# Full attention: PSUM banks and distances of the two matmul streams that run ahead

## The reference, cut to what matters

```
x = x + attn(_layernorm(x), Wq, bq, Wk, bk, Wv, bv, Wo, bo)      # _L1_attn_b_ref
def proj(W, b):
    return (jnp.einsum('btc,oc->bto', x, W) + b).reshape(Bb, Tt, H, D).transpose(0, 2, 1, 3)
q = _rope(proj(Wq, bq)); k = _rope(proj(Wk, bk)); v = proj(Wv, bv)
scores = jnp.einsum('bhtd,bhsd->bhts', q, k) / jnp.sqrt(D)
attn = jax.nn.softmax(scores, axis=-1)
out = jnp.einsum('bhts,bhsd->bhtd', attn, v)
out = out.transpose(0, 2, 1, 3).reshape(Bb, Tt, C)
return jnp.einsum('btc,oc->bto', out, Wo) + bo
```

## Time and profile before

| | us |
|---|---|
| median of 3 runs | 4485.8 |
| lowest, highest | 4483.82, 4503.86 |
| profiled execution, its own time | 4470.18 |
| span of its trace | 4468.4 |
| full attention in it, first maxima matmul to last values (3464 to 4118) | 654 |
| part with scores (3500.3 to 4118) | 617.7 |
| one frame of 64 slots, full clock | 78.8 |

### The profile page before, as it was taken

One profiled execution on the slowest core, in us unless ns is written; L12 is line 12 of the kernel. 1 busy time (PEld: TensorE's weight loads), 2 busy tenths in 40 slices (PEclk: granted clock), 3 DMA queues, 4 the chain that ended last, 5 costly groups with the idle time before them and its releaser, 6 DMA issues. The chain is left out here.

```text
span 4468.4 us, 60003 instructions
## 1 busy us (share of the span) xinstructions
PE 3753.4 (84%) x19225; PEld 2607.0 (58%) x19288; DVE 2864.8 (64%) x5347; ACT 1912.2 (43%) x3864; POOL 1567.3 (35%) x1463
## 2 busy tenths in 40 slices
PE   5888878799499999988898588885886888888898
PEld 3555557688488888877787244443663333333566
DVE  6676557565555555547565478777885566664898
ACT  3454543343355555453343344532221355555232
POOL 4565526444566655436443111100001443330000
PEclk8898989899799999989899688997998799998999
DMA  6987912454100000002454200000001544450000
GB/s 171 270 240 229 271 40 71 145 163 150 43 11 12 17 13 11 1 17 73 152 168 142 65 19 19 19 1 15 0 0 36 102 98 84 96 102 16 9 10 19
DMA packets 221651, 348.37 MB, mean 78 GB/s; under 512 B 34632, under 2 KB 126266, under 8 KB 215226
## 3 DMA queue, kind: packets, MB, share of 16 engines
q1 hardware_dynamic: 198714, 260.66, 19.8%
q0 software_dynamic: 22656, 84.24, 8.3%
HBM read 166.29 MB, written 169.87 MB: 75 GB/s over the span
## 5 line engine op out<-in xcount | busy, mean ns | idle before, releaser
L2771 DVE TENSOR_REDUCE ab_nmx<-banks 128x1 f32<-128x512 f32 x512 | 334.7, 686 | 208.1 <-PE banks L2587 207.3
L2713 ACT ACTIVATE ab_pt<-banks 128x512 f32<-128x512 f32 x512 | 273.7, 600 | 90.2 <-PE banks L2597 77.4
L1664 POOL TENSOR_TENSOR lb_pq<-lb_pq,lb_rr 128x512 f32<-128x512 f32 x192 | 203.9, 1065 | 307.1 <-DVE lb_rr L1543 304.1
L2597 PE MATMUL banks<-ab_qT,ab_kT 49*128 49x512 f32 x512 | 227.5, 491 | 54.9 <-ACT ab_pt L2713 52.9
L1418 ACT ACTIVATE lb_pq<-banks,lb_nmx 128x256 f32<-128x256 f32 x384 | 178.9, 471 | 220.5 <-DVE lb_nmx L1538 217.6
L2587 PE MATMUL banks<-ab_kT,ab_qT 48*128 48x512 f32 x512 | 235.4, 508 | 30.7 <-DMA ab_kT<-ab_spill 19.1
L1538 DVE TENSOR_REDUCE lb_nmx<-banks 128x2 f32<-128x512 f32 x192 | 131.5, 685 | 185.2 <-PE banks L1270 184.2
L2597 PEld LDWEIGHTS banks<-ab_qT,ab_kT 49*128 49x128 f32 x512 | 92.2, 194 | 261.6 <-ACT ab_pt L2713 158.5
L634 POOL DMA_INDIRECT mb_xi<-moe_ys,moe_b_place x64 | 63.6, 995 | 390.3 <-DVE mb_uT L2045 342.7
L2825 POOL DMA_DIRECT2D ab_kT<-in_ab_ones x4 | 2.1, 548 | 525.0 <-POOLq L2978 525.0
L566 POOL TENSOR_TENSOR da_pt<-da_pt,w_da_tri 128x384 f32<-128x384 f32 x128 | 144.8, 1131 | 111.0 <-ACT da_pt L350 110.8
(11 more groups left out here) (561 smaller groups left out, 11480.3 us busy)
## 6 DMA issues: line engine op xcount, KB each, us to landing
moe_xs<-zero SPq DMA_DIRECT2D x71, 512.0 KB, 11.1
moe_ys<-zero SPq DMA_DIRECT2D x71, 512.0 KB, 10.9
moe_a_w_raw<-in_moe_w SPq DMA_DIRECT2D x48, 512.0 KB, 3.9
moe_b_w_raw<-in_moe_w SPq DMA_DIRECT2D x48, 512.0 KB, 3.8
da_spill<-da_hi SPq DMA_DIRECT2D x128, 128.0 KB, 2.4
ab_spill<-ab_hi SPq DMA_DIRECT2D x128, 128.0 KB, 2.4
da_qT<-da_spill POOLq DMA_DIRECT2D x32, 384.0 KB, 7.3
da_kT<-da_spill POOLq DMA_DIRECT2D x32, 384.0 KB, 10.3
```

The lines of the kernel that those rows point to most:

```text
L1664: nc.gpsimd.tensor_tensor(pq[:, n % RING, :, :], pq[:, n % RING, :, :], bcast(rr[:, n % RING, :], 2, 2 * P), ALU.mult).then_inc(s_p, 1)
L2597: nc.tensor.matmul(ps[:, EXP_BANK + n % 3, :], kT[b % 2][r:r + AB_ROWS + 1, p, j * P:(j + 1) * P], qT[b % 2][r:r + AB_ROWS + 1, p, :], sta ...
L2713: nc.scalar.activation(pt[:, s % RING, :], ps[:, EXP_BANK + s % 3, :], ACT.Exp, scale=AB_D ** -0.5).then_inc(s_e, 1)
L2771: nc.vector.tensor_reduce(nmx[:, g % 2, col:col + 1], ps[:, MAX_BANK + n % 3, :], op=ALU.max, axis=AX.X, negate=True).then_inc(s_mx, 1)
```

## The change

Two banks for maxima and four for scores instead of three and three. The waits follow the number of banks, TensorE issues scores one slot further ahead (s+3), and LEAD goes from 37 to 38. Nothing else is different.

```diff
-    LEAD = 37
+    LEAD = 38
     RING = 8
     NV = NS // 4
-    MAX_BANK, EXP_BANK, SUM_BANK, ODD_BANK = 0, 3, 6, 7
+    MAX_BANK, EXP_BANK, SUM_BANK, ODD_BANK = 0, 2, 6, 7
+    NMAX, NEXP = 2, 4
...
-                    if n >= 3:
-                        pe.wait_ge(s_mx, n - 2)
-                    nc.tensor.matmul(ps[:, MAX_BANK + n % 3, :], ...
+                    if n >= NMAX:
+                        pe.wait_ge(s_mx, n - NMAX + 1)
+                    nc.tensor.matmul(ps[:, MAX_BANK + n % NMAX, :], ...
...
-                    if n >= 3:
-                        pe.wait_ge(s_e, n - 2)
-                    nc.tensor.matmul(ps[:, EXP_BANK + n % 3, :], ...
+                    if n >= NEXP:
+                        pe.wait_ge(s_e, n - NEXP + 1)
+                    nc.tensor.matmul(ps[:, EXP_BANK + n % NEXP, :], ...
...
-                    if 0 <= s + 2 < NS:
-                        scores(s + 2)
+                    if 0 <= s + NEXP - 1 < NS:
+                        scores(s + NEXP - 1)
...
-                        nc.scalar.activation(pt[:, s % RING, :], ps[:, EXP_BANK + s % 3, :], ACT.Exp,
+                        nc.scalar.activation(pt[:, s % RING, :], ps[:, EXP_BANK + s % NEXP, :], ACT.Exp,
...
-                        nc.vector.tensor_reduce(nmx[:, g % 2, col:col + 1], ps[:, MAX_BANK + n % 3, :], op=ALU.max,
+                        nc.vector.tensor_reduce(nmx[:, g % 2, col:col + 1], ps[:, MAX_BANK + n % NMAX, :], op=ALU.max,
```

More of the change, by code:

```diff
@@ L2584, in maxima @@
                             pe.wait_ge(s_stack[i], stack_all * (2 * b + g // 2 + 1))
-                    if n >= 3:
-                        pe.wait_ge(s_mx, n - 2)
-                    nc.tensor.matmul(ps[:, MAX_BANK + n % 3, :], qT[b % 2][r:r + AB_ROWS, p, qt * P:(qt + 1) * P],
+                    if n >= NMAX:
+                        pe.wait_ge(s_mx, n - NMAX + 1)
+                    nc.tensor.matmul(ps[:, MAX_BANK + n % NMAX, :], qT[b % 2][r:r + AB_ROWS, p, qt * P:(qt + 1) * P],
                                      kT[b % 2][r:r + AB_ROWS, p, :], start=True, stop=True).then_inc(s_m, 1)
@@ L2594, in scores @@
                         pe.wait_ge(s_shift[n // 16 % 2], shift_all * (n // 32 + 1))
-                    if n >= 3:
-                        pe.wait_ge(s_e, n - 2)
-                    nc.tensor.matmul(ps[:, EXP_BANK + n % 3, :], kT[b % 2][r:r + AB_ROWS + 1, p, j * P:(j + 1) * P],
+                    if n >= NEXP:
+                        pe.wait_ge(s_e, n - NEXP + 1)
+                    nc.tensor.matmul(ps[:, EXP_BANK + n % NEXP, :], kT[b % 2][r:r + AB_ROWS + 1, p, j * P:(j + 1) * P],
                                      qT[b % 2][r:r + AB_ROWS + 1, p, :], start=True, stop=True).then_inc(s_s, 1)
```

## The result

The changed kernel takes 4548.99 us in the median of 4 runs, against 4494.83 us in the median of 4 of the kernel before: ratio 1.0123, 95% interval 1.0099 to 1.0147, about 54 us slower. The direction was forecast, at half the size: 28 us and 4514 were predicted, and the range ended at 4536.

A forecast was written before the change was run, and what follows sets the result against it. TensorE's strict order, with each stop of its queue, was taken as the bound. Terms 20 + 5.4 + 1.5 + 3 - 2.7 = +27, with small waits +28, on the median 4485.8 gave 4514 us; 8-in-10 range 4497 to 4536.

The forecast's parts named there:

- plain groups: Four slots without odd jobs: third maxima wait for the first reduction, 2.74 us becomes 3.34, +0.60 each.
- v job: Slots 26 to 29: the job's first load follows the later third maxima, +0.85 us, nothing behind recovers it.
- end of the frame: Slots 62 to 65: the turn beside GpSimd's operation ends earlier, maxima of slot 65 go sooner, -0.3 us.
- tail: The 38 slots without maxima: values to values 2.22 us instead of 2.60, -2.7 us in all, from 0 to -8.
- heads, out and qk groups: Groups with these jobs: a job or ScalarE's emptying separates the pairs long enough, so the change costs 0.
- Before the first scores: Maxima ahead of any scores go 0.79 us apart instead of 0.60: +3 us, from 0 to +5.
- The fourth scores bank: Scores issued one slot earlier: TensorE's stops costed at 0 where maxima remain; only the tail gains.
- After the statistics: Slots 18 to 21: maxima of slot 21 go 2.20 us later, much given back at slot 22, +0.6 us.
- Rival 1: More half clock from TensorE standing in plain groups, in all seven frames instead of three: 4530 us, chance 0.16.
- Rival 2: Price partly covered: earlier scores save stops, the start is hidden, the tail keeps full clock: 4500 us, chance 0.17.
- Rival 3: Scores decide, maxima don't: plain groups fall from 2.74 to 2.40 us, 4473 us in all, chance 0.07.
- Rival 4: Each slot's two matmuls use different halves as before, so a pair costs the same: 0, no time of its own.

The follow-up runs named there:

- experiment 2: Two banks for maxima, three for scores, scores two slots ahead, LEAD 37, against the kernel before: ratio 1.0136.
- experiment 8: Two banks for maxima, three for scores, LEAD 37, statistics moved to slots 28 to 30, against the kernel before: ratio 1.0011.
- experiment 3: The changed kernel with the statistics moved from slot 18 to slots 28 to 30: ratio to the kernel before 0.9995, 4484.85 us.
- experiment 6: The kernel before with LEAD 38 alone, three and three banks: ratio 1.0713, 4812.99 us.
- experiment 1: The kernel before with one wait tightened: slot 21's maxima wait for the reduction two slots back instead of three; ratio 1.0048, 4510.9 us.
- experiment 7: The kernel before with LEAD 39 alone, three and three banks: ratio 1.001, 4503.3 us.
- experiment 9: The kernel before with statistics moved to slots 28 to 30 and a frame's last turn from slot 61 to 62: ratio 0.9942, 4454.15 us.

## Why the prediction was wrong

- *The waits, right.* Measured, and predicted in brackets: plain groups 3.33 (predicted 3.34), with a shift 3.38 (3.37), v job, at full clock, 5.09 for 4.25 (+0.84; +0.85), end of the frame 3.82 for 4.11 (-0.3), back jobs +0.04 (0.05), tail 2.27 (2.22), heads, out and qk groups unchanged where the clock was full. Before the first scores +2.4 us (41.0 for 38.6; +3). The waits of a frame come to 3.5 (3.35), 0.6 of it not measured.
- *The fourth scores bank, right.* It gives nothing to speak of but in the tail: 1.0136 without it and 1.0123 with it, and the full-clock frame is 80.0 either way (experiments 2 and 8).
- *After the statistics, the failed step.* "Much of it is given back ... +0.6" holds for the wait alone. The stand of 2.20 us itself was costed only as a delay. In every frame of the changed kernel from the second on TensorE was at 1.2 GHz behind it, mostly for 13.7 us, which stretched the groups to slots 21, 25 and 29. A second, short fall of 3.4 us at slots 37 to 45 adds some 1.5 in four of them; what brings it is open. Together it is a frame of 88.7 where the waits give 82.3, 6.4 us a frame. The last frame, with the tail, is 7.7 us longer, where the sum gave 1.2 less; it has 34 us at half clock instead of 11. That fall is not the stand's, as it comes ahead of it, and its cause is open. Taking the stand away takes 55.9 us off the stage (experiment 3), of which the two waits for VectorE at slot 22, present before as well, are 1.6 a frame.
- *Rival 1, the right mechanism at the wrong place and size.* It named the half clock, but it put it at the plain groups' stands of 0.8 us, as one more stretch in four frames, 16 us and a chance of 0.16. It was one in each frame, at the longest stand. There was a sign to read: the kernel before has its stand of 1.3 us at the end of the frame, and in two of its slow frames, from 3737.3 and from 3819.4, the slow group lies behind that one (to slot 5, 8.19 for 6.61). It was a weak sign, since the same stand in the other frames left the clock at 1.00. The rule of the Trainium skill that is cited there, in "TensorE: Matmul & The Clock Gate", section "A second HAM failure mode: psum-queue depth-cycling", says that frequent short idles between matmul groups make the clock fall and rise. The traces agree in part: the clock does fall and rise behind idle times of 1 to 2 us, but the frames of experiment 3 have all the short ones and three of them kept 1.00, in a stage with 30 us at half clock, where with the one long stand a frame it was 149.
- *Rivals 2 and 3* are out. Rival 3 needed the third maxima early, and they came at 1.31. Rival 2 needed the start to be hidden, ScalarE's stops to shrink and the tail to keep its clock: the start cost 2.4, the heads, out and qk groups kept their lengths at full clock, and the half clock in the last frame grew. *Rival 4* is right for the change: the two matmuls of a slot still load at the same time (3889.26). Where a distance puts them on the same half, it costs 7% (experiment 6).

## What to carry to other kernels

Price a new wait twice: by what it delays, and by how long it leaves TensorE without a matmul. In this kernel 2.2 us of standing were reckoned at 0.6 us in delays and cost some 2 us (experiment 1, in the median) to 6 us (the changed kernel's profile) more at 1.2 GHz behind it. Look for VectorE's longest job in the order, as that is where a bank less turns into a long stand. Of two producers ahead of their readers, give the bank to the one whose reader comes last in the wait (here maxima, 1.31 us from a load until its bank is free for the next, where three can be issued in 0.34). Keep streams that share TensorE's rows in turn on opposite halves whenever a distance is changed.

## What the runs showed of the hardware

- TensorE at 2.4 GHz for 30.4 us, then 1.71 us without a matmul, was at 1.2 GHz for the next 13.7 us, though busy 12.9 us of them. In the changed kernel and in experiments 1 and 2, 18 times of 1.71 us without a matmul began at full clock, and each has a fall between 1.1 us before its end and 1.9 us behind it. It is not what every fall needs: in the last frame of the changed kernel the clock fell at 4153.9 with no time over 0.83 us without a matmul in the 10 us before.
- Matmuls of 48 and 49 rows one behind the other on the same half, 98% busy by the windows of two frames of experiment 6, ran at 0.51 and 0.55 of the clock; the same matmuls in pairs on both halves, in the kernel before and in experiment 7, at 0.96 and more.
- VectorE's product of two SBUF operands takes 0.68 alone and 1.80 beside a GpSimd product (ending 0.55 after it); in experiment 9, where it stands later in the order and only 0.3 us of GpSimd's work is left beside it, it takes 0.85. The Trainium skill, "SBUF — State Buffer", section "Who interferes with whom", says that a VectorE instruction with two SBUF inputs contends with a GpSimd instruction that reads SBUF; the trace agrees.
